# Start of a fused attention and expert kernel: scales broadcast straight from the input, their power of two applied with the codes, and the second batch's layer norm spread among the first projections

## The reference, cut to what matters

```python
x = L0_attn_a_hidden_states                       # (2, 512, 512) f32
x = x + _L0_attn_a_ref(_layernorm(x), ...)        # 32 heads of 128, 8 KV heads, 4-bit codes with scales
x = x + _L0_ffn_ref(_layernorm(x), ...)           # top 2 of 8 low-rank experts
x = x + _L0_attn_b_ref(_layernorm(x), ...)        # 32 heads of 16
x = x + _L0_ffn_ref(_layernorm(x), ...)

def _dequant(codes, scales):
    w = codes.astype(jnp.float32) - 8.0
    return w * jnp.repeat(scales, GS, axis=0)
# in attention A
q = hidden_states @ _dequant(q_codes, q_scales)   # k and v likewise; then rotary, causal softmax, @ v
return out @ _dequant(o_codes, o_scales)
```

## Time and profile before

| what | us |
|---|---|
| median of 3 runs | 1159.73 (1156.37 to 1162.29) |
| the profiled execution's own time | 1155.95 |
| its span in the trace | 1154.1 |
| mean granted TensorE clock, share of full | 0.982 |
| TensorE busy | 1019.4 |
| VectorE busy | 902.5 |
| ScalarE busy | 706.9 |
| GpSimd busy | 683.6 |

### The profile page before, as it was taken

How to read it: one execution, slowest core, us unless ns; L and a number is a source line. 1 busy time by engine, 2 the same in 40 slices (tenths; PEclk the granted TensorE clock), 3 DMA queues, 4 the chain that set the end, 5 groups by cost and what they waited for, 6 DMA issues and landing times.

```text
span 1154.1 us, 25383 instructions
## 1 busy us (share of the span) xinstructions
PE 1019.4 (88%) x8608; PEld 631.0 (55%) x8608; DVE 902.5 (78%) x2021; ACT 706.9 (61%) x1561; POOL 683.6 (59%) x808
## 2 busy tenths in 40 slices
PE   1688999999999999999999978798777777777898
PEld 1345555555555555555555534455466666666554
DVE  5777877877778877877778876787779999999755
ACT  2157666666656666656666553346778888888331
POOL 3678786777678767867776514465445555555211
PEclk9999999999999999999999999899989999999999
DMA  7065354735744753555566350000000000000001
GB/s 275 16 178 142 109 139 122 170 80 137 179 118 80 191 122 74 170 142 139 108 128 156 92 127 11 1 1 1 1 1 2 0 0 0 0 0 0 1 1 73
DMA packets 180268, 94.94 MB, mean 82 GB/s; under 512 B 168288, under 2 KB 169056, under 8 KB 175584
## 3 DMA queue, kind: packets, MB, share of 16 engines
q1 hardware_dynamic: 170832, 50.85, 20.8%
q10 hardware_dynamic: 9360, 43.01, 11.4%
HBM read 49.64 MB, written 2.26 MB: 45 GB/s over the span
## 4 chain that ended last, share of the span: by engine, by line
PE 70%; ACT 11%; DVE 7%; issue 5%; POOL 3%; DMA 2%; SPq 0%; ACTq 0%; DVEq 0%; POOLq 0%
PE bank L942 14%; PE bank L944 14%; PE bank L943 14%; ACT prob L705 5%; PE bank L1273 5%; ACT ptb_hi L712 3%; PE bank L1240 3%; PE bank L1023 3%; PE bank L1024 3%; PE bank L1025 3%; PE bank L1044 3%; PE bank L1046 3%; PE bank L1045 3%; DVE xn L1364 2%; PE bank L1026 1%
## 5 line engine op out<-in xcount | busy, mean ns | idle before, releaser
L478 POOL TENSOR_TENSOR rt<-rt 128x512 f32<-128x512 f32 x80 | 101.0, 1266 | 157.6 <-DVE rt L1441 157.6
L1488 DVE SCALAR_TENSOR_TENSOR bw_hi<-bank,rden,bw_hi 128x128 f16<-128x128 f32 (+3 forms) x256 | 123.3, 544 | 60.4 <-ACT bw_hi L722 60.4
L694 ACT ACTIVATE bank<-bank,shift,c_score 128x128 f32<-128x128 f32 (+3 forms) x256 | 147.1, 604 | 2.1
L705 ACT ACTIVATE prob<-bank,shift,c_score_b 128x128 f32<-128x128 f32 (+3 forms) x256 | 137.5, 632 | 0.0
L722 ACT ACTIVATE bw_hi<-bank,rden 128x128 f16<-128x128 f32 (+3 forms) x256 | 114.0, 529 | 32.8 <-DVE rden L1481 32.8
L1455 DVE TENSOR_REDUCE smax<-bank 128x1 f32<-128x512 f32 (+3 forms) x256 | 109.3, 484 | 26.1 <-PE bank L1026 24.6
L1465 DVE TENSOR_REDUCE smax<-bank 128x1 f32<-128x128 f32 (+3 forms) x256 | 113.4, 485 | 18.7 <-PE bank L1245 16.4
L1240 PE MATMUL bank<-kt_b,qt_b 128*128 (+4 forms) x256 | 72.1, 308 | 53.7 <-ACT prob L705 53.5
L689 ACT ACTIVATE shift<-smax,c_score 128x4 f32<-128x4 f32 x64 | 19.0, 297 | 158.9 <-DVE smax L1455 158.9
L634 POOL TENSOR_TENSOR shift<-smax,c_score_b 128x1 f32<-128x1 f32 (+1 forms) x192 | 36.6, 191 | 110.3 <-DVE smax L1465 101.8
L942 PE MATMUL bank<-xt_hi,wq_hi 128*128 128x512 f16 x256 | 98.4, 384 | 3.4 <-DVE rt L1441 2.2
(11 more groups left out here) (217 smaller groups left out, 3227.4 us busy)
## 6 DMA issues: line engine op xcount, KB each, us to landing
qcode<-in_q_codes ACTq DMA_DIRECT2D x8, 1024.0 KB, 4.9
qscale<-scales_q ACTq DMA_DIRECT2D x7, 1024.0 KB, 7.6
ocode<-in_o_codes ACTq DMA_DIRECT2D x7, 1024.0 KB, 5.0
oscale<-scales_o ACTq DMA_DIRECT2D x7, 1024.0 KB, 8.4
kvcode<-in_k_codes ACTq DMA_DIRECT2D x8, 256.0 KB, 7.9
kvcode<-in_v_codes ACTq DMA_DIRECT2D x8, 256.0 KB, 8.3
x<-in_x SPq DMA_DIRECT2D x2, 1024.0 KB, 7.1
out<-x SPq DMA_DIRECT2D x8, 256.0 KB, 2.0
```

The lines of the kernel that those rows point to most:

```text
L694: act.activation(a_rows(i, s), a_rows(i, s), ACT.Exp, bias=shift[:, s % 2, c:c + 1], scale=c_score[:, 0:1], accum_out=bank[3][:, SUMS_AT + ...
L705: act.activation(prob[:, i2, S_OFF[i]:S_OFF[i] + w], bank[bk][:, o:o + w], ACT.Exp, bias=shift[:, i2, c:c + 1], scale=score[:, 0:1]).then_ ...
L1488: dve.scalar_tensor_tensor(out=p_row[:, s % 2, LO_AT[i]:LO_AT[i] + P_STEP * i + 1:P_STEP], in0=turned_back(i, s), scalar=rden[:, s % 2, c: ...
```

## The change

- SP no longer stores scaled scales. `load_scales` spreads the unscaled scales straight from the input, in every group; the scratch tensors, DVE's multiplication of `scn` (L1378), the four stores and the waits for them are gone.
- The power of two goes into the codes: `codes` on ACT is now `Identity` with per-partition operands, scale `inv_q` and bias `eight_q` = -8 `inv_q`, in place of `Copy` with bias -8. For k and v it is two instructions instead of one. This holds for every group.
- x's first four tiles come by one transfer each, the first ahead of the scales; x's second half is issued behind the constants; kv's and q's scales of group 0 are issued from ACT's queue behind their codes, with no wait among them, and o's scales and codes from SP's. ACT runs one small `Exp` before its first use of codes.
- DVE takes the statistics of the first four tiles ahead of `power_of_two`.
- On ACT the codes of kv and q stand ahead of all `ln_hi`; o's codes move into group 0 behind `rope_hi(0, ("q", 2))`.
- The second batch's tiles: statistics and normalisation of tiles 4 and 5 stand on DVE among the first batch's `ln_lo`; their transposes on PE behind `project(0, "k", 0)` and `project(0, "q", 0)`; tiles 6 and 7 move into group 0, behind `("q", 2)` and `("q", 3)`. `LN_BANK` gives them banks 6 and 7. `("k", 0)` needs only `xt_done` of the first batch; `("q", 3)` waits for six tiles and `("k", 1)` for all eight.
- DVE's two `first_q` stand behind `rope(0, ("q", 0))` and behind `rope(0, ("q", 1))`. A start projection of q waits for its own slice of the weights only.
- POOL's `deq_kv(0, 1, 3)`, the v weights, stands behind the three start ropes, and these in the order add, low, add, low, add, low.

```diff
-LN_BANK = [(0, 1), (2, 3), (3, 4), (3, 4)]
+LN_BANK = [(0, 1, 0, 1, 6, 7, 6, 6), (2, 3) * 4, (3, 4) * 4, (3, 4) * 4]
...
-                              scr[n][bass.ds(j * 2048, 2048)].partition_broadcast(P)).then_inc(d_wscale[n], 16)
+                              t_in[f"{n}_scales"][bass.ds(j * 2048, 2048)].partition_broadcast(P)).then_inc(d_wscale[n], 16)
...
+            sp.dma_start(x[:, 0], x_in[:, 0]).then_inc(d_x[0], 16)
...
-            sp.dma_start(x[:, 0:ST, :], x_in[:, 0:ST, :]).then_inc(d_x[0], 16)
+            for t in range(1, ST):
+                sp.dma_start(x[:, t], x_in[:, t]).then_inc(d_x[t], 16)
...
-            sp.wait_ge(scn_done, 4)
-            for n in QUANT:
-                w = QUANT_COLS[n]
-                sp.dma_start(scr[n].rearrange("(p f) -> p f", p=P), scn[:, off:off + w]).then_inc(d_scr, 16)
-                off += w
-            sp.wait_ge(d_scr, 64)
-            load_scales(sp, "kv", 0)
-            sp.dma_start(x[:, ST:NT, :], x_in[:, ST:NT, :]).then_inc(d_x[1], 16)
-            for n in "qo":
-                load_scales(sp, n, 0)
+            sp.dma_start(x[:, ST:NT, :], x_in[:, ST:NT, :]).then_inc(d_x[ST], 16)
+            load_scales(sp, "o", 0)
             load_codes(sp, "o", 0)
...
             deq_kv(0, 0, 0)
...
             deq_q(0, 1, 2)
+            rope_add(0, ("k", 0))
+            rope_lo(0, ("k", 0))
+            rope_add(0, ("q", 0))
+            rope_lo(0, ("q", 0))
+            rope_add(0, ("q", 1))
+            rope_lo(0, ("q", 1))
             deq_kv(0, 1, 3)
-            start()
             group(0, 0, False)
...
+                for i, m in enumerate(n):
+                    c = QUANT.index(m)
+                    src, dst = (code[:, i], code_f[:, i]) if n == "kv" else (code[:], code_f[:])
+                    last = act.activation(dst.rearrange("p a b -> p (a b)"), src.rearrange("p a b -> p (a b)"),
+                                          ACT.Identity, bias=eight_q[:, c:c + 1], scale=inv_q[:, c:c + 1])
+                last.then_inc(done, 1)
 
             load_codes(act, "kv", 0)
-            act.wait_ge(scn_done, 4)
+            load_scales(act, "kv", 0)
             load_codes(act, "q", 0)
...
+            load_scales(act, "q", 0)
+            act.wait_ge(consts, 2)
+            act.activation(rsum[:, 0, 0:1], one[:], ACT.Exp).then_inc(act_ready, 1)
+            act.wait_ge(eight_done, 1)
+            codes(0, "kv", kvcode, kvcode_f, d_code["kv"], 32, kv_code)
+            codes(0, "q", qcode, qcode_f, d_code["q"], 16, q_code)
+            for t in range(ST):
                 ln_hi(0, t)
-            codes(0, ocode, ocode_f, d_code["o"], 16, o_code)
...
                 rope_hi(j, ("q", 2))
+                if first:
+                    codes(0, "o", ocode, ocode_f, d_code["o"], 16, o_code)
+                    ln_hi(0, ST + 2)
                 next_kv_q(j, last)
...
                 rope_hi(j, ("q", 3))
+                if first:
+                    ln_hi(0, ST + 3)
...
-            for name in AHEAD:
-                rope_hi(0, name)
+            ln_hi(0, ST)
+            rope_hi(0, ("k", 0))
+            ln_hi(0, ST + 1)
+            rope_hi(0, ("q", 0))
+            rope_hi(0, ("q", 1))
             group(0, True, False)
...
-            for t in range(NT):
+            for t in range(ST):
                 ln_t(0, t)
-            pe.wait_ge(chain, 3)
             pe.wait_ge(xt_done, ST)
...
-                    pe.wait_ge(q_w, 4 * j + (4 if place == "start" else s + 1))
-                if (kind, s) == ("q", 0) and place == "start":
+                    pe.wait_ge(q_w, 4 * j + s + 1)
+                if (kind, s) == ("q", 3) and place == "first":
+                    pe.wait_ge(xt_done, ST + 2)
+                if (kind, s) == ("k", 1) and place == "first":
                     pe.wait_ge(xt_done, NT)
...
                 project(j, "q", 2, place)
+                if first:
+                    ln_t(0, ST + 2)
...
                 project(j, "q", 3, place)
+                if first:
+                    ln_t(0, ST + 3)
...
-            for kind, s in AHEAD:
-                project(0, kind, s, "start")
+            project(0, "k", 0, "start")
+            ln_t(0, ST)
+            project(0, "q", 0, "start")
+            ln_t(0, ST + 1)
+            project(0, "q", 1, "start")
+            pe.wait_ge(chain, 3)
             group(0, 0, "first")
...
             for t in range(ST):
-                ln_lo(0, t)
-                if t + 2 < ST:
-                    ln_norm(0, t + 2)
-            dve.wait_ge(d_x[1], 16)
+                dve.wait_ge(d_x[t], 16)
+                ln_stats(0, t)
+            power_of_two(pow_q, inv_q, slice(0, 4), redq, invq_done)
+            dve.tensor_scalar(eight_q[:], inv_q[:], -8.0, None, ALU.mult).then_inc(eight_done, 1)
+            ln_norm(0, 0)
+            ln_norm(0, 1)
+            for t in range(2, ST):
+                ln_lo(0, t - 2)
+                ln_norm(0, t)
+            dve.wait_ge(d_x[ST], 16)
             for t in range(ST, ST + 2):
                 ln_stats(0, t)
-            for t in range(ST, ST + 2):
+                ln_lo(0, t - 2)
                 ln_norm(0, t)
...
+            for t in range(ST + 2, NT):
+                ln_stats(0, t)
+            ln_lo(0, ST)
...
                 probs_low(j, 0)
+                if first:
+                    ln_lo(0, ST + 2)
+                    ln_norm(0, ST + 3)
...
                 probs_low(j, 1)
+                if first:
+                    ln_lo(0, ST + 3)
...
-            for name in AHEAD:
-                rope(0, name)
+            rope(0, ("k", 0))
+            ln_lo(0, ST + 1)
+            ln_norm(0, ST + 2)
+            rope(0, ("q", 0))
+            first_q(0)
+            rope(0, ("q", 1))
+            first_q(1)
             group(0, True, False)
```

More of the change, by code:

```diff
@@ L652, in ln_hi, with codes @@
                 act.activation(xt_hi[:, :, t * P:(t + 1) * P],
-                               bank[LN_BANK[c][t % 2]][:].rearrange("p (k n) -> p k n", k=KT),
+                               bank[LN_BANK[c][t]][:].rearrange("p (k n) -> p k n", k=KT),
                                ACT.Copy, scale=X_UP).then_inc(xthi_done, 1)
-            def codes(j, code, code_f, loaded, count, done):
+            def codes(j, n, code, code_f, loaded, count, done):
                 act.wait_ge(loaded, count)
-                act.activation(code_f[:].rearrange("p a b -> p (a b)") if len(code_f.shape) == 3 else
-                               code_f[:].rearrange("p i a b -> p (i a b)"),
-                               code[:].rearrange("p a b -> p (a b)") if len(code.shape) == 3 else
-                               code[:].rearrange("p i a b -> p (i a b)"), ACT.Copy, bias=-8.0).then_inc(done, 1)
+                for i, m in enumerate(n):
[4 more added lines that the diff above has]
+                last.then_inc(done, 1)
             load_codes(act, "kv", 0)
-            act.wait_ge(scn_done, 4)
+            load_scales(act, "kv", 0)
             load_codes(act, "q", 0)
-            codes(0, kvcode, kvcode_f, d_code["kv"], 32, kv_code)
-            ln_hi(0, 0)
-            codes(0, qcode, qcode_f, d_code["q"], 16, q_code)
-            for t in range(1, NT):
+            load_scales(act, "q", 0)
[5 more added lines that the diff above has]
+            for t in range(ST):
                 ln_hi(0, t)
-            codes(0, ocode, ocode_f, d_code["o"], 16, o_code)
             def rope_hi(j, name):
@@ L949, in ln_t @@
                 if i >= 2:
-                    pe.wait_ge(xt_done, i - 1)
+                    pe.wait_ge(xt_done, i - (i != NT - 1))
                 for k in range(KT):
-                    mm = pe.transpose(bank[LN_BANK[c][t % 2]][:, k * P:(k + 1) * P],
+                    mm = pe.transpose(bank[LN_BANK[c][t]][:, k * P:(k + 1) * P],
                                       xn[:, t % 2, k * P:(k + 1) * P], ident[:])
@@ L1399, in first_q @@
                 dve.tensor_tensor(wq_lo[:, :, c], qcode_f[:, :, c], wq_hi[:, :, c], ALU.subtract).then_inc(q_w, 1)
[L1401 to L1405 removed]
+            off = 0
+            dve.wait_ge(d_scale, 64)
+            for i, n in enumerate(QUANT):
+                w = QUANT_COLS[n]
+                dve.tensor_reduce(amax_q[:, i:i + 1], scn[:, off:off + w], AX, ALU.max,
+                                  apply_absolute_value=True).then_inc(amaxq_done, 1)
+                off += w
+            for t in range(ST):
+                dve.wait_ge(d_x[t], 16)
[8 more added lines that the diff above has]
+            dve.wait_ge(d_x[ST], 16)
             for t in range(ST, ST + 2):
                 ln_stats(0, t)
[L1408 removed]
+                ln_lo(0, t - 2)
                 ln_norm(0, t)
[L1410 to L1418 removed]
+            dve.wait_ge(d_const, 16 * N_CONST)
+            dve.tensor_copy(ident_h[:], ident[:]).then_inc(chain, 1)
+            dve.tensor_copy(ident_b[:], ident[:]).then_inc(chain, 1)
```

(4 more changed lines are left out.)

61 lines of the change are left out of this document (10 added, 51 removed).

## The result

The changed kernel takes 1161.67 us (median of 20 runs, 1158.70 to 1162.98) where the kernel before takes 1159.28 (20 runs, 1155.95 to 1162.29): ratio 1.0022, interval 1.0015 to 1.0030. It is slower by some 2.5 us, a little, but measurably. The forecast was 1158.4, a gain of 1.3. The profiled execution of the changed kernel took 1161.83, that of before 1155.95, the fastest of its 20.

A forecast was written before the change was run, and what follows sets the result against it. PE's order sets the time from head 4 (90.71), so only lead left there counts: 13.7 us at the first k projection shrinks to 1.3. 1155.95 - 1.3 = 1154.65 profiled, 3.78 below the median: 1158.4; range 1151 to 1162.

The forecast's parts named there:

- the first of the prediction's sum: Start, up to the first normalised tile: removing multiplication, stores and wait gains nothing there; tile at about 15.1 as before.
- this switch of POOL: POOL's unexplained idle time between reduction and reciprocal roots, 6.71 us, taken to recur unchanged, with roots at about 14.5.
- The slower rival: At the start: competing loads bring x's second half late, up to 23.5, making the median up to 1162.0; chance 0.22.
- From the root to head 4 the steps: First k near 24, q1 40.5, maxima of heads 0 to 2 at 51.8, 63.4, 72.0, head 4's scores 89.4.
- q1 at the lower clock level: q1's projection on PE, after about 6 us idle, runs at 1.2 GHz and takes 5.3 us, to 45.8.
- the clock's rival: PE runs first k and q1 at the higher level, keeping 5.5 us of lead, median 1154.2; chance 0.17.
- The first k projection as slow as before: PE's first k projection again runs at the lower clock level and takes 5.3 us.
- Tile 6 waits on ACT behind o's codes: Before head 1's maxima: o's codes, 1.9 us, delay tile 6; maxima at 63.4 against 63.32, lead gone.
- x's second half in time: Load at the start, needed at 19.9, expected between 15 and 23.5 and taken as causing no wait.
- `codes` in the full stretches costs nothing: After head 4: one more ACT instruction for k and v, under 0.3 us, beside PE's full stretches.
- `Identity` and the table: Rival on ACT: `Identity` shares no table with `Exp`, so conversions reload, 61 us, giving 1186; chance 0.02.

The follow-up runs named there:

- e4: Kernel before with only the change's loads, unscaled scales, `Identity` codes and early statistics, otherwise in the old order; +6.0 us, ratio 1.0053.
- e1: Changed kernel, with ACT issuing its loads, all but the first codes, only once the four small scale copies have landed; ratio 1.0024.
- e2: Changed kernel, holding x's second half and ACT's loads except the first codes until the first root, q's codes behind `ln_hi`; ratio 1.0045.
- e9: Kernel before, with only the load of x's second half moved ahead of the wait for the scaled scales; ratio 1.0017.
- e6: As e5, but o's codes are converted on ACT at the start, ahead of group 0; ratio to the kernel before 1.0024.
- e5: Changed kernel with ACT's k and v loads as in e1, and q's and o's loads held until the first root; ratio 1.0025.
- e11: As e5, with x's second half also held until the first root, so only k's and v's scales go; ratio 1.0039.
- e10: e3 with o's codes early, q0's rope ahead of tile 5, and both `first_q` ahead of q1's rope; median 1155.41, ratio 0.9970.
- b2: The kernel before, unchanged, run and profiled a second time; ratio 1.0002.
- e3: Kernel before with only the change's new order (second batch's norm, `first_q`, v weights, ropes, o's codes), loads and codes as before; ratio 1.0007.
- e8: e3 with x's second half issued behind the constants, and o's codes taken early with o's scales behind them; ratio 1.0010.
- e7: Changed kernel without POOL's reduction of the scales' maximum over partitions; DVE copies its own maxima instead; ratio 1.0002.

## Why the prediction was wrong

**The step that failed** is the first of the prediction's sum: "I cost the removal there at nothing; the cover is this switch of POOL", with the first normalised tile "at about 15.1 as before". The switch was taken as a constant, since two rows of it, 6.71 and 6.88, agreed; but they agree under the transfers of the kernel before, which are not those of the change. With the loads of the change it is 9.17, and the small copies ahead of it land 5.4 us later. The later gap stays near 7 (6.84 to 7.29) in all 13 kernels that have the first reduction, also where the first one is 9 to 12; it told nothing of the first one under other loads. In the row of 6.88 the profile names DVE's `mv` as what ended the wait, but the first tile's `mv` was done at 683.92, 2.1 us before the roots, so that gap isn't one of data either. The root came at 21.14 and not at 14.5. e4 shows that the loads alone do this, e1 that the copies alone don't explain it, e2 and e9 that the loads also act on the gap itself.

**The slower rival** had the right kind of cause, loads that come late because everything competes at once, and the wrong place. It was priced by x's second half at tile 4, for which DVE never had to wait. Its bound of 1162.0, inside which the result lies, therefore came from another transfer than the one that was late.

**The rule of the Trainium skill** that I drew on (DMA: Bandwidth & Descriptors, Issuing engines are not separate DMA queues) was used for the sum of the megabytes only. That the transfers of ACT's queue interleave with SP's small copies is the same rule, and speaks against the change: a copy that took 3.0 us took 7.9. The Trainium skill (DMA: Bandwidth & Descriptors, Queues, rings and completion order) also says that each DMA engine goes round the queues it has work for packet by packet. e1, where the copy takes 3.2 us again once ACT's queue is held, fits with that; no run here shows the order of the packets.

**From the root to head 4 the steps held.** Predicted and measured, in us:

| step | predicted | measured |
|---|---|---|
| root to first k projection | 9.3 | 10.2 |
| first k to q1 | 16.7 | 16.6 |
| q1 to head 0's maxima | 11.3 | 10.3 |
| head 0 to head 1 | 11.6 | 10.7 |
| head 1 to head 2 | 8.6 | 8.4 |
| head 2 to POOL's sum for k | 5.1 | 5.1 |
| sum to head 4's scores | 12.3 | 12.3 |
| together | 74.9 | 73.7 |

So the whole miss at head 4, 94.82 for 89.4, is 6.6 late at the root less 1.2 in these steps. In these, `first_q` before head 0, taken as 3.9, lasted 3.0 from 55.25 on, near its lower bound, and the step to head 1 was 0.9 shorter; the way to the first k projection was 0.9 longer, 0.8 of it ahead of tile 4's statistics. With the prediction's 74.9 us put behind the true root head 4 would come at 96.0, 5.3 late; by the profile it is 4.1 late, and by the median the kernel is 2.4 slower.

**By point.** q1 at the lower clock level: right (matmuls of 0.61 us at 47.90, granted clock 0.50 from 47.9 to 53.2), so the clock's rival fell. The first k projection as slow as before: right; it lasts 5.2, its matmuls 0.63 or less. But that this is the lower level was read from the durations alone, and the granted clock doesn't show it: it is 1.00 from 31 to 37 us, and before it was 1.00 from 37 to 43. Tile 6 waits on ACT behind o's codes, and head 1 has no lead left: right (2.11 us at 65.26, DVE waits 2.00 for the high part). But e6 shows that taking these codes away gains nothing, because q3's projection is next. x's second half in time: right on the late root only. It landed at 20.7 (8.96 + 11.7) and was first used at 27.31; at the root I forecast it was due at 19.9, and would have cost some 0.8 if it had landed at the same time. `codes` in the full stretches costs nothing: right. PE's busy time there is the same within 0.2 us of 382, though ACT is busy 3.5 us more. *`Identity` and the table*: one load of 1.28 us in the whole execution, so nothing reloads; the Trainium skill's statement (ScalarE: Activation LUTs, Table sets: the hidden batching unit) that identity is in every table set agrees with this trace.

**What stays open.** Why the gap behind the reduction depends on the transfers. It isn't bandwidth during the gap alone: before has 283 GB/s in it and 6.71 us, e9 323 GB/s and 9.16. Nor does it wait for the queues to drain: in e5 nothing moves from 18 to 20 us and the root still comes only at 19.82, while in e1 it comes at 21.12 with the engines full until 24. In e2, e11 and e5 the gap grows with what is let through, but by no measure that I found for all kernels (11.97 in e1, 9.17 in the changed kernel with as much in the queues), and what POOL fetches in it no row shows. Nor is it settled why the median is 1.7 us less late than head 4; the two profiles of before show that the rest alone can vary by as much.

## What to carry to other kernels

Idle time "on issue" that no data explains is no constant: read what lies in the DMA queues when it begins, and look for it at another load before you let a removed wait release megabytes into it. A wait in front of big loads may be what keeps a small transfer on the critical path fast; let the small one land first, but look at what comes behind it: in e1 the gap took back all that the early copies gave. Hold only what nobody needs soon (e2 and e11 show how holding too much comes back). When work is moved forward in an in-order queue, check next which instruction in front of the bank's release is not needed for it: here that order (e10) was worth 3.6 us, while none of the kernels with earlier loads was faster than the one before.

## What the runs showed of the hardware that was not expected

- POOL's gap between the reduction over partitions and the roots: 6.7 to 7.1 us in before, b2, e2, e3 and e10; 8.05 with 0.5 MB of scales in the queues (e11); 9.0 to 12.0 with x's second half or more (after, e1, e4, e5, e6, e8, e9). Late in the execution, with 94 GB/s moving, it was 6.88, and 7.19 in the changed kernel with 91; in all kernels but e7 it was 6.84 to 7.29 there, in e1 6.84 behind a first gap of 11.97. A like gap stands ahead of the first reduction, 7.47 in e1 and 6.22 in e9, and 6.1 to 7.8 in all kernels whose copies are early enough to show it.
- A copy of 64 KB took 3.0 us from issue to landing, and 7.9 with 3 MB in another engine's queue. The 1 MB of x's second half took 11.7 in the changed kernel.
- In the changed kernel, with two queues full, a DMA share of about 1.0 meant 192 GB/s from 6 to 8 us, where the small copies and the spread scales of k and v were in it, and 370 to 426 in the stretches of 2 us from 8 to 24. In e5, where the small copies had landed by 5.9 us, it was still only 197 from 10 to 12, with a share of 0.96 and k's and v's spread scales on their way. In stretches of 1 us the changed kernel reached 461 (10 to 11), no less than the 451 of the earlier trace rows.
